# A two-layer attention and FFN chain on one core: where the second attention's joined weights and keys are made, how the first attention builds its stacked queries and keys, and which PSUM banks it uses

## What is computed

```python
x = x + _L0_xattn_ref(_layernorm(x), ctx, mask, Wq, bq, Wk, bk, Wv, bv, Wo, bo)
...
x = x + _L0_ffn_ref(_layernorm(x), ...)            # 16 experts, best 4 per row
...
x = x + _L1_xattn_ref(_layernorm(x), ctx, Wq, bq, Wk, bk)
```

```python
Q = einsum('btx,dx->btd', text, Wq) + bq
K = einsum('bpx,dx->bpd', features, Wk) + bk
attn = softmax(einsum('btd,bpd->btp', Q, K) * scale)
attended = einsum('btp,bpd->btd', attn, features)
```

## Time and profile before

| | us |
|---|---|
| median of 3 runs | 1108.66 |
| the three runs | 1106.32, 1108.66, 1112.56 |
| the profiled execution's own time | 1106.41 |
| its span, first to last instruction | 1104.5 |
| PE busy | 953.8, 86% of the span |
| DVE, ACT and POOL busy | 64%, 42% and 35% of the span |
| stretch 0 to 177.3, the first attention | 177.3 |
| stretch 177.3 to 258.0, norm, router and shared expert | 80.7 |
| stretch 258.0 to 510.2, the 47 tiles | 252.2 |
| stretch 510.2 to 579.0, keys, picks, second attention | 68.8 |
| stretch 579.0 to 1104.5, the rest | 525.5 |

### The profile page before, as it was taken

How to read it: one execution, slowest core, us unless ns; L and a number is a source line. 1 busy time by engine, 2 the same in 40 slices (tenths; PEclk the granted TensorE clock), 3 DMA queues, 4 the chain that set the end, 5 groups by cost and what they waited for, 6 DMA issues and landing times. The chain is left out here.

```text
span 1104.5 us, 14956 instructions
## 1 busy us (share of the span) xinstructions
PE 953.8 (86%) x4939; PEld 616.9 (56%) x4939; DVE 702.7 (64%) x1178; ACT 458.6 (42%) x672; POOL 381.3 (35%) x368
## 2 busy tenths in 40 slices
PE   5888884998999999999887588899987698679997
PEld 2555542655666666665354344455464455457886
DVE  5677547396777677873968853476635788445334
ACT  2445432324656566662225332344502465335130
POOL 5244203104755566662321320211120122048431
PEclk9899865899999999999987899699988899979999
DMA  8000102234978867655504100000003100032001
GB/s 317 1 1 2 58 1 96 82 134 120 346 281 302 347 243 259 226 193 182 189 1 182 39 1 0 20 2 1 1 1 150 51 1 1 0 96 77 29 11 39
DMA packets 32988, 112.69 MB, mean 102 GB/s; under 512 B 4304, under 2 KB 4624, under 8 KB 29840
## 3 DMA queue, kind: packets, MB, share of 16 engines
q1 hardware_dynamic: 25392, 87.08, 21.6%
q0 software_dynamic: 7520, 24.65, 6.7%
HBM read 132.69 MB, written 16.78 MB: 135 GB/s over the span
## 5 line engine op out<-in xcount | busy, mean ns | idle before, releaser
L1208 POOL DMA_INDIRECT f_picks<-f_turn_xn,f_target x47 | 110.4, 2350 | 76.8 <-ACT f_turn_xn L1097 76.5
L1624 PE MATMUL banks<-f_t_dn,f_z 128*128 128x512 f32 x188 | 88.5, 593 | 0.6 <-issue 0.6
L1352 DVE TENSOR_TENSOR f_gu_lo<-f_t_gu,f_gu_hi 128x2048 fp32r<-128x2048 f32 x24 | 55.1, 2297 | 15.6 <-ACT f_gu_hi L1083 13.6
L1202 POOL DMA_INDIRECT f_turn_xn<-f_xn_rows,f_token x47 | 48.4, 1030 | 43.6 <-DVE f_token L1346 18.7
L1352 DVE TENSOR_TENSOR f_xn_lo<-f_t_gu,f_xn_hi 128x2048 fp32r<-128x2048 f32 x23 | 52.7, 2292 | 14.6 <-ACT f_xn_hi L1083 14.6
L2322 ACT ACTIVATE a_e<-banks 128x1024 f32<-128x1024 f32 x32 | 32.8, 1025 | 54.7 <-PE banks L2414 54.7
L2352 DVE TENSOR_REDUCE a_mx<-banks 128x8 f32<-128x1024 f32 x32 | 39.1, 1222 | 23.2 <-PE banks L2394 23.2
L1090 ACT ACTIVATE f_sil<-banks 128x256 f32<-128x256 f32 x47 | 18.1, 384 | 80.3 <-PE banks L255 80.3
L1083 ACT CAST f_gu_hi<-f_t_gu 128x2048 fp32r x24 | 45.7, 1904 | 10.7 <-DMA f_t_gu<-in_f_gu 7.9
L164 PE MATMUL banks<-ident,f_turn_xn 128*128 128x128 f32 x96 | 21.5, 377 | 32.6 <-DVE f_turn_xn L172 32.5
L1083 ACT CAST f_xn_hi<-f_t_gu 128x2048 fp32r x23 | 43.7, 1902 | 10.6 <-DMA f_t_gu<-in_f_gu 7.7
(11 more groups left out here) (416 smaller groups left out, 2598.8 us busy)
## 6 DMA issues: line engine op xcount, KB each, us to landing
f_t_gu<-in_f_gu SPq DMA_DIRECT2D x47, 1024.0 KB
f_t_dn<-in_f_dn SPq DMA_DIRECT2D x47, 512.0 KB
f_t_gu<-f_picks SPq DMA_DIRECT2D x8, 1024.0 KB, 5.1
f_xn_rows<-f_turn_xn SPq DMA_DIRECT2D x9, 256.0 KB, 2.5
x_res<-in_x SPq DMA_DIRECT2D x8, 256.0 KB, 7.7
a_ctx<-in_ctx SPq DMA_DIRECT2D x2, 1024.0 KB, 13.8
a_out_mask<-in_mask SPq DMA_DIRECT2D x1, 2048.0 KB, 15.9
a_ct<-in_ctx_turned SPq DMA_DIRECT2D x4, 512.0 KB, 8.4
```

The lines of the kernel that those rows point to most:

```text
L1202: pool.indirect_dma_start(t_rows[:, t % F0_BUFS, :], None, dram["f0_xn_rows"], bass.IndirectOffsetOnAxis(ap=token[:, t:t + 1], axis=0))\
L1208: pool.indirect_dma_start(dram["f0_picks_flat"], bass.IndirectOffsetOnAxis(ap=target[:, t:t + 1], axis=0), t_y[:, t % F0_BUFS, :], None).t ...
L1352: dve.tensor_tensor(t_gu_lo[t % 2], t_gu[:, bass.ds(i, 1), :, :].rearrange("p i c n -> p (i c n)"), t_gu_hi[t % 2].bitcast(F32), ALU.subtr ...
L1624: mm = pe.matmul(ps[:, TY_BANK + t % 2, :], t_zt[:, t % 2, c, :], t_dn[:, t % F0_BUFS, c, :], start=c == 0, stop=c == F0_IC - 1)
```

## The change

**First attention.** One projection per batch makes queries and keys together (64 and 64 rows, L776). DVE adds bias and mask (`keys_queries`, L688), ACT takes the upper part (`upper_part`, L619), POOL the lower (`lower_part`, L521). SP writes five pieces per batch to a DRAM buffer `a0_parts` and reads the stack back in four DMAs (`store`, `fetch`); mask and ones rows stand there already. Three stack buffers are zeroed by POOL, three batches are projected ahead. POOL takes over `normalise` of batches 3 to 7, ACT the copy of the values (their bias moves into GELU). Masks and context come per batch. Scores have banks 4 and 5, the keyed scores banks 6 and 7, each pair alternating its two halves with what reads it, and PE's list interleaves them:

```diff
+                    for b in range(A0_EARLY):
+                        project(b)
+                    scores(0)
+                    scores(1)
+                    join_vectors()
                     for u in range(UNITS + 1):
-                            keyed(2 * u)
-                            keyed(2 * u + 1)
+                            turn_max(u)
+                            scores(2 * u + 2)
+                            keyed(2 * u - 1)
+                            project(batch_at(u))
+                            project_values(values_at(u))
+                        fill(u, range(0, 2))
                             values(u - 1)
-                            project_values((u + 1) // 2)
-                            scores(2 * u + 2)
                             scores(2 * u + 3)
+                            keyed(2 * u)
+                        fill(u, range(2, 3))
                             turn_outputs(u - 1)
-                            project(u + 3)
-                            turn_max(u + 1)
+                        fill(u, range(3, 4))
...
+                    def scores(s):
+                        pe.wait_ge(st_loaded[b % A0_BUFS][s % 2], 16 * 2 * (b // A0_BUFS + 1))
+                        if s >= 1:
+                            pe.wait_ge(max_ready, s)
...
+                    def keyed(s):
+                        if s >= 1:
+                            pe.wait_ge(exp_ready, s)
```

**The second attention's preparation** moves into the first attention. ACT issues the loads of both weights at the start. `join_vectors` makes the bias vectors by 36 float32 products, 32 of them with a single moving column:

```diff
+                    def join_vectors():
+                        pe.wait_ge(j_loaded, 48)
+                        for i, w in enumerate((j_wk, j_wq)):
+                            for c in range(NC):
+                                for d in range(NC):
+                                    pe.matmul(ps[:, JOIN_BANK, at:at + 1], w[:, d, c * P:(c + 1) * P],
+                                              j_bias[:, i, d:d + 1], start=d == 0, stop=d == NC - 1)
```

```diff
-                for n in range(HALVES * KEY_JOBS):
-                    for c in range(NC):
-                        keys(n, c)
...
-                    join_biases(t)
...
-                        for k, (out, src) in enumerate(halves(a_ct[:, h, :, :]..., dram["ctx_turned"][h])):
+                        for k, (out, src) in enumerate(halves(a_kt[:, h, :, :]..., dram["a1_keys"][h]...)):
...
-                    pe.wait_ge(a_keys_ready, KEY_JOBS * (half + 1))
+                    pe.wait_ge(a_kt_loaded[half], 32)
+                    pe.wait_ge(a_row_loaded, 16)
```

DVE's new list ahead of the first maximum, and in a unit:

```diff
+                    keys_queries(0)
+                    statistics(1)
+                    statistics(2)
+                    dve.tensor_tensor(qk_lo[:, 0, :], ...)
                     normalise(1)
+                    keys_queries(1)
+                    normalise(2)
+                    keys_queries(2)
                     maximum(0)
                     maximum(1)
...
+                        divide(u - 2); maximum(2 * u + 2); statistics(...); keys_queries(...)
+                        lower(u); maximum(2 * u + 3)
```

More of the change, by code:

```diff
@@ new lines, in l0_attention, with keys_before @@
+            j_keys_ready, j_row_ready = core.sem("a1_keys_ready"), core.sem("a1_row_ready")
+            j_keys_stored = [core.sem(f"a1_keys_stored_{i}") for i in range(2)]
+            j_row_stored = core.sem("a1_row_stored")
+            JOINED = [("joined", m, None) for m in range(NC)]
+            for h in range(HALVES):
+                JOINED += [("keys", m, h) for m in range(NC)] + [("row", 0, h)]
+            def keys_before(n):
+                return sum(kind == "keys" for kind, _, _ in JOINED[:n])
@@ L384, in _ @@
[L384 to L390, removed]
-                    sp.dma_start(wo[:, :], dram["a0_wo"]).then_inc(loaded, 16)
@@ new lines, in _ @@
+                    for b in range(3, B):
+                        if b + 1 < B:
+                            load_mask(b + 1)
+                        load_ctx(b)
+                        store(b)
+                        fetch(b)
+                        if b == HB:
+                            sp.dma_start(j_ct[:, 1, :, :].rearrange("p c n -> p (c n)"), dram["ctx_turned"][1])\
+                              .then_inc(j_ct_loaded[1], 16)
+                    sp.dma_start(wo[:, :], dram["a0_wo"]).then_inc(loaded, 16)
@@ new lines, in _ @@
+                    pool.memset(mx[:, :, :], 0.0).then_inc(mx_zeroed, 1)
+                    pool.memset(j_row_w[:, :, :], 0.0)
+                    pool.memset(j_shift[:, :], 0.0).then_inc(j_zeroed, 1)
+                    for b in range(1, 3):
+                        first.scale(pool, b)
+                    pool.wait_ge(cols_ready, 1)
+                    keep_rows(1)
+                    lower_part(1)
+                    clear(1)
+                    keep_rows(2)
+                    lower_part(2)
@@ L412, in _ @@
+                    for i in range(2):
+                        pool.memset(v[:, i, :, :, :], 0.0).then_inc(zeroed, 1)
+                    pool.wait_ge(zeroed, 2)
                     for i in range(2):
                         pool.memset(v[:, i, :, :, A0_DH:A0_DH + 1], 1.0).then_inc(zeroed, 1)
-                    first.scale(pool, 0)
-                    pool.wait_ge(cols_ready, 1)
-                    pool.wait_ge(first_mask_loaded, 16)
-                    for b in range(1, 3):
+                    clear(2)
@@ L539, in divide @@
+                        if b >= 2:
+                            dve.wait_ge(qk_lo_ready, b - 1)
+                        dve.scalar_tensor_tensor(out=qk[:, b % 2, :], in0=ps[:, QK_BANK, :],
+                                                 scalar=cols[:, C_B:C_B + 1], in1=kept[:, b % 2, :], op0=ALU.add,
+                                                 op1=ALU.mult).then_inc(qk_ready, 1)
                     def divide(u):
@@ new lines, in join @@
+                    def join(m, parts):
+                        if 0 in parts:
+                            if m == 0:
+                                pe.wait_ge(j_vec_ready, 1)
+                            else:
+                                pe.wait_ge(j_joined_ready, m)
+                        for d in parts:
+                            mm = pe.matmul(ps[:, JOIN_BANK, :], j_wk[:, d, m * P:(m + 1) * P], j_wq[:, d, :],
+                                           start=d == 0, stop=d == NC - 1)
+                        if NC - 1 in parts:
+                            mm.then_inc(j_done, 1)
@@ L710, in _, with fill @@
+                    def fill(u, parts):
+                        if joined_at(u) is not None:
+                            job(joined_at(u), parts if JOINED[joined_at(u)][0] != "row"
+                                else range(NC) if 0 in parts else range(0))
                     pe.wait_ge(first_loaded, 16)
+                    for b in range(A0_EARLY):
+                        project(b)
                     pe.wait_ge(const_ready, 4)
-                    project(0)
-                    project(1)
```

651 lines of the change are left out of this document (328 added, 323 removed).

## The result

The change makes the kernel slower: 1135.46 us median of 4 runs (1134.9 to 1139.01) against 1107.49 for the kernel before in the same session, a ratio of 1.0237 with a 95% interval of 1.0197 to 1.0278. The profiled execution took 1134.94, its span is 1132.8, so 28.3 us longer than the 1104.5 of before. The forecast was 1106, no change, with a range of 1095 to 1119; the change costs 28 us.

What follows compares the result with a forecast made beforehand. The prediction took PE to bound the first attention's units, and DVE's picks the end of the tiles. Its terms, +4.0 (first three), -1.4, -2.4 and 0, gave +0.2 on 1106.4: forecast 1106 us, own range 1101 to 1112, stated range 1095 to 1119.

Steps and rivals of the forecast that it cites:

- Term 1: Start, up to the first turn of the maxima: it moves from 22.80 to 37.0, +14.2 us, bounds 34.0 to 42.0.
- Term 2: The 14 filled units of the first attention: 104.1 us in all, about 7.4 per unit, no less than before.
- Term 3: Units 14 and 15, without jobs and bound by latency: 16.5 us to the end of the last turn.
- Term 4: Joins leaving the FFN: of 14.1 us of PE only 0.7 to 1.9 is on the path, so -1.4 us.
- Term 5: Tiles 9 to 19: mainly nine DVE steps and their reads leave, -2.4 us, bounds -1.9 and -3.45.
- Term 6: Behind the last tile: 34.8 us of keys and row products leave PE, covered by DVE's picks; 0, plus or minus 1.
- Rival B: Slower through PE's low clock: two more half-clock spells (+7.2) and all vectors at low level (+6.9), giving 1120 us; 26%.

Runs made afterwards that it cites:

- e1: The changed kernel with the loads of masks 1 and 2 issued ahead of the first store: 1128.83 us median, 1.0179 times the kernel before.
- e5: The kernel before with only the new first attention, masks early, no bias vectors or jobs, old FFN: 1107.95 us median, 0.9976 times the kernel before.
- e4: The changed kernel with three of the four products of each join and keys job left out: 1115.55 us median.
- e8: As e5, with x 3 and mask 3 loaded ahead of the first fetch, later masks one batch earlier: 1100.2 us median, 0.9904 times the kernel before.
- e6: The kernel before with one product instead of four in each keys and row job behind the last tile: 1110.01 us median, 1.0003 times the kernel before.
- e3: The changed kernel with 56 unread products added where the joins and keys stood before: 1130.69 us median.
- e7: As e2, with the unread products of e3 added in the FFN: 1119.15 us median.
- e2: As e1, with the bias vectors ahead of the first scores in PE's list: 1119.71 us median, 1.0068 times the kernel before.
- e9: As e2, with the 36 products of the bias vectors made a second time in unit 14, results unread: the second set took 12.2 us.

## Why the prediction was wrong

**Term 1, the start (+14.2 forecast, +27.5 measured): the step that failed.** The forecast was 10.8 us for the vectors and 3.4 for everything else that is new ahead of the first turn. The vectors began at 36.3 and not at 26.2, 10.1 us late, for two reasons.

First, I took the masks "in at about 15". They were issued at 17.75 and in at 24.5: the first store begins only at 12.35, when ACT has its upper part, its five pieces take over half a us of SP's queue each and one 1.84, and a load then took 6.7 us with the DMA engines 78% busy in this stretch. From there on the links were right: masks to vectors 11.8 us measured, 11.2 forecast. With the masks early the vectors begin at 30.7 (e1), 5.6 us sooner.

Second, the chain has no term at all for the stack's way through DRAM: five stores, four fetches, and PE's first scores behind them. It runs beside the masks' chain and takes over when that is short: in e1 PE waits 9.3 us for it, and the first scores are at 27.1, later than 26.2, where I had them done. The other 4.5 of the 10.1 us stay with it.

Then the vectors took 13.7 us instead of 10.8: 3. I had PE return to the high level of its clock after 4.2 us, from what it did before; here all of the set ran at the low one. Both of my prices were too high, 0.246 for 0.21 at the low level and 0.13 for 0.11 at the high one, which hid part of that (and 17 x 0.246 + 55 x 0.13 is 11.3, not 10.8). Bound and all, 50.3 lies far outside my 34 to 42.

The pieces by experiment: the masks' order 5.6 us (e1), the vectors 13.0 (44.75 there, 31.76 in e5 with neither vectors nor their loads), and 9.0 for the rest of the new start (31.76 against 22.80), in which PE waits 9.0 for the stack. They add up to the 27.5, rounding apart, because each is the difference of two neighbouring traces.

**Term 2, the units: right.** 104.1 us for 14 units was forecast, 108.2 measured (50.32 to 158.54). 2.4 of the difference is the first unit, most of it still at the low level (9.81 instead of 7.4), 1.7 one unit of 9.56 in a spell of low clock. The other twelve average 7.40, where the forecast's 104.1 / 14 is 7.44. The row jobs overlap: their units take 6.04 and 5.42. What I drew from it was too kind: "no less than before" hides that 19 to 23 of these us (e4, e8) were a price for moving work that was covered (e6) into a stage that PE bounds.

**Term 3, the drain:** 16.5 forecast, 19.4 measured (158.54 to 177.90), beyond my slow bound of 18.5. PE's mean granted clock was 0.62 there. Before, the same two units took 19.2 us (134.44 to 153.64), which I could have read.

**Term 4, the joins out of the shared expert: wrong in sign.** -1.4 forecast, +1.0 measured. The joins stood in DVE's shadow, and in their place PE idles and its clock falls; e3 gives the 1.0 back.

**Term 5, tiles 9 to 19:** -2.4 forecast, -3.5 measured there (55.15 to 51.67), the far bound. Over all tiles it is -2.4 as well, but by luck: the tiles behind lost 1.1 again. Part of the 3.5 is spread between executions, since e6, with the tiles of the kernel before, needs 53.4 for the same ten.

**Term 6, the tail: right.** 0, plus or minus 1; the change is +1.0 there, and e6 shows that the keys held nothing: 30.37 us from first pick to first maxima in the change, as before.

Of the 28.1 us between forecast and result 13.3 are term 1, 7.0 terms 2 and 3, 2.4 term 4, 0.6 the way out, 1.4 the tail. The last 3.4 lie behind the next layer's norm, in code that the change doesn't touch. Before, the change and e1 to e7 have 521.9 to 529.7 us there, e6 the longest, so I count them as the spread of executions. Rival B named the right sign and a low clock for the vectors, for which it had 6.9 us where 2.9 came, but not the waits that made most of the loss; its spells in the units came once, for 1.7 us. It is no hit.

## What to carry to other kernels

Ask first which engine bounds the stage that work is moved into: keys that lay behind VectorE's picks for nothing, and joins that cost nothing either, are paid at about 20 us for 31 in a stage whose unit is PE's own sum. Then walk the start of a kernel queue by queue: each DMA that an engine waits for has an issue time set by everything ahead of it on its queue, and a load behind a store waits for all that the store waits for. List every path that ends at the first unit, not the longest one alone: when e1 shortened the masks' path, the stack's took over. Small work ahead of the first unit is paid in full unless it lies in such a wait (e2), and here it ran at the low level of the clock.

## What the runs showed of the hardware

- PE's work for nobody is not quite without use: 16 float32 products of 512 columns, unread, in place of idling keep the granted clock at 1.00 where it was 0.74 to 0.83, and the shared expert is 1.0 us shorter. Forty more during the picks keep it at 1.00 instead of 0.50 and gain nothing measurable.
- Float32 products with one moving column and 128 weight columns stand 0.11 us per instruction apart at the high level and 0.21 at the low one (e9, and the start of the change).
- A view's granted 1.00 at the start of a kernel need not be a record: in the change the first record of the clock is at 57.5 us, and the rows ahead of it run at half speed (a turn of the maxima 1.12 us at 50.32, 0.60 at 60.13).
- The stack's way through DRAM, five stores and four fetches, takes 16.8 us from the first store's issue to the first scores (9.91 to 26.73 in e5), of which PE waited 9.0.
